# Five stacked loads a slot instead of ten, and a new order on every engine, in a one-layer decoder kernel

## The reference

```python
x = x + attn(_layernorm(x), w_qkv, w_o)              # B=4, T=512, D=512, 16 heads of 32, causal, rotary
x = x + ssm(ctx_1024, _layernorm(x), in_proj_w, ...) # selective scan, 512 channels, 16 states
x = x + ffn(_layernorm(x), w_fc, w_proj)             # 512 -> 2048 -> 512, ternary weights, GELU
# in the ssm, for each batch:
u = silu(conv(in_proj(ctx)) + conv_b);  dt, B, C = x_proj(u);  delta = softplus(dt_proj(dt) + b)
state = state * exp(delta * A) + (delta * u) * B;  y = sum_n state * C + D * u
out = y * silu(z)                                    # z is the layer-normed x after attention
```

## Time and profile before

| | |
|---|---|
| time, median of 3 runs (lowest, highest) | 1005.8 us (1002.96, 1011.9) |
| the profiled execution, own time | 1006.11 us |
| its span | 1004.2 us |
| mean granted TensorE clock | 0.964 |
| busy: TensorE, VectorE, ScalarE, GpSimd | 91%, 86%, 75%, 61% |

### The profile page before, as it was taken

How to read it: one execution, slowest core, us unless ns; L and a number is a source line. 1 busy time by engine, 2 the same in 40 slices (tenths; PEclk the granted TensorE clock), 3 DMA queues, 4 the chain that set the end, 5 groups by cost and what they waited for, 6 DMA issues and landing times.

```text
span 1004.2 us, 17516 instructions
## 1 busy us (share of the span) xinstructions
PE 913.4 (91%) x5476; PEld 605.8 (60%) x5476; DVE 859.1 (86%) x1167; ACT 757.1 (75%) x1490; POOL 617.6 (61%) x439
## 2 busy tenths in 40 slices
PE   6979898888999999989898998877999998999998
PEld 4455665666686676776666677765854554554444
DVE  4698979999999999889898678998898898899731
ACT  4987746755569878687989774996499999989660
POOL 0266927666461867687555787344579878797520
PEclk9989899999999999999999999788999999999999
DMA  5757766856564665343535466423036846574535
GB/s 167 247 190 236 215 202 206 252 165 216 158 210 141 186 209 168 113 146 103 161 96 154 120 178 246 154 64 121 6 68 153 175 98 132 121 148 84 106 74 125
DMA packets 148857, 153.57 MB, mean 153 GB/s; under 512 B 93008, under 2 KB 97360, under 8 KB 148512
## 3 DMA queue, kind: packets, MB, share of 16 engines
q1 hardware_dynamic: 148768, 152.46, 53.9%
HBM read 103.00 MB, written 28.44 MB: 131 GB/s over the span
## 4 chain that ended last, share of the span: by engine, by line
PE 41%; ACT 20%; DVE 18%; issue 12%; POOL 6%; DMA 2%; SPq 0%; ACTq 0%; DVEq 0%; POOLq 0%
PE ps L1749 6%; PE ps L1818 5%; PE ps L1875 5%; DVE hb L1895 4%; ACT p_q L1599 4%; PE ps L1830 4%; ACT ps L1486 4%; PE ps L1762 4%; PE ps L1792 4%; DVE y_acc L1917 3%; POOL hb L1366 3%; PE ps L1865 2%; ACT L1467 2%; PE ps L1773 2%; ACT p_t L1615 2%
## 5 line engine op out<-in xcount | busy, mean ns | idle before, releaser
L1366 POOL TENSOR_TENSOR hb<-du,b_bc 128x1024 f32<-128x1024 f32 (+1 forms) x160 | 307.0, 1939 | 156.7 <-PE ps L1818 156.3
L1895 DVE TENSOR_TENSOR_SCAN hb<-ps,hb 128x1024 f32<-128x1024 f32 (+1 forms) x128 | 257.2, 2015 | 20.7 <-ACT ps L1486 17.9
L1486 ACT ACTIVATE ps<-delta,a_neg 128x511 f32<-128x511 f32 (+2 forms) x320 | 179.5, 600 | 87.0 <-DVE hb L1895 81.1
L1917 DVE SCALAR_TENSOR_TENSOR y_acc<-ps,ct,y_acc 128x512 f32<-128x512 f32 x256 | 179.3, 737 | 21.4 <-PE ps L1818 21.0
L1818 PE MATMUL ps<-ident,hb 128*128 128x128 f32 x1088 | 152.0, 282 | 30.1 <-DVE hb L1895 15.9
L1818 PEld LDWEIGHTS ps<-ident,hb 128*128 128x128 f32 x1088 | 127.2, 145 | 60.6 <-issue 18.6
L1599 ACT ACTIVATE p_q<-ps,m_col 128x512 f32<-128x512 f32 (+3 forms) x256 | 132.0, 540 | 18.5 <-DVE m_col L1992 18.1
L1749 PE MATMUL ps<-xn_t,w_ring 128*128 128x512 f32 x256 | 118.0, 604 | 1.9 <-ACT p_q L1599 1.3
L1865 PE MATMUL ps<-t_fc,xt 128*128 128x512 f16 x512 | 117.1, 382 | 0.8 <-ACT h_sb L1663 0.7
L1875 PE MATMUL ps<-t_pr,ht 128*128 128x512 f16 x512 | 112.8, 379 | 1.0 <-DVE y_acc L1917 1.0
L1792 PE MATMUL ps<-ident,p_q 128*128 128x128 f32 x640 | 91.7, 295 | 8.8 <-ACT p_q L1599 6.0
(11 more groups left out here) (137 smaller groups left out, 1529.2 us busy)
## 6 DMA issues: line engine op xcount, KB each, us to landing
w_ring<-in_w_attn SPq DMA_DIRECT2D x32, 512.0 KB, 4.0
qk_d<-hl SPq DMA_DIRECT2D x64, 256.0 KB
q_st<-qk_d SPq DMA_DIRECT2D x128, 128.0 KB, 2.8
b_bc<-bc_d SPq DMA_DIRECT2D x48, 256.0 KB, 3.7
raw<-in_w_fc SPq DMA_DIRECT2D x16, 512.0 KB, 5.2
raw<-in_w_pr SPq DMA_DIRECT2D x16, 512.0 KB, 5.8
k_st<-qk_d SPq DMA_DIRECT2D x64, 128.0 KB, 2.7
k_st<-qk_d SPq DMA_DIRECT2D x128, 64.0 KB, 2.3
```

What stands on the lines that cost most here:

```text
L1366: nc.gpsimd.tensor_tensor(piece_of(e, hi, lo).rearrange("p (a n) -> p a n", a=2), du[b % 2][:, 2 * h:2 * h + 2, lo:hi], b_bc[:, i % BC_RIN ...
L1486: ins = nc.scalar.activation(factors(j, hi, lo)[:, (hi - lo) * m + start:(hi - lo) * (m + 1)], delta[b % 2][:, et, lo + start:hi], ACT.Exp ...
L1895: v.tensor_tensor_scan(h, d, h, 0.0, ALU.mult, ALU.add).then_inc(scan_done, 1)
L1917: v.scalar_tensor_tensor(out=y, in0=bank(kind, r, tb), scalar=ct[:, b % 2, tb, n:n + 1], in1=y, op0=ALU.mult, op1=ALU.add).then_inc(y_free ...
```

## The change

Each `stack` item issued five loads for each of its two heads. Now each of the five carries both heads, with the same bytes and the same rows of 2 KB, and the wait in front of the scores counts 80 where it counted 160. The planner learns that an issue keeps SyncE busy (0.46 us, and more for some kinds), where it had 0.1 us; two first loads get their real number of transfers; the factor on TensorE's and VectorE's durations goes from 1.03 to 1.02. One wait is added to the first `ln1b` copy of a batch on ScalarE, since the new order can put the last `rot` of the batch before behind the last `v`. All tables of due times have new numbers, by which every engine's order is another. What each item computes is unchanged.

```diff
-WEIGHT = {'pe': {'ln1b': 1.9,
+WEIGHT = {'pe': {'ln1b': -40.55,
...
-ATTN = [{'stack': [-7.0],
+ATTN = [{'stack': [-158.25],
...
-SWITCH = 17.35
+SWITCH = 42.4
...
+ISSUE, ISSUES = 0.46, {"xt": 1.3, "ht_ffn": 2.0, "stack": 3.4, "lo": 2.7}
...
-        yield "act", 0.5, [pe(*item)] + ([pe("v", b - 1, 1, 1)] if b else [])
+        yield "act", 0.5, [pe(*item)] + ([pe("v", b - 1, 1, 1), pe("rot", b - 1, 3, 1)] if b else [])
...
-        yield "sp", 4, [pe("inproj", a[0] - 1, ET - 1)] if a[0] else []
+        yield "sp", 4 if a[0] else 8, [pe("inproj", a[0] - 1, ET - 1)] if a[0] else []
...
-    slow = {"pe": 1.03, "dve": 1.03}
+    slow = {"pe": 1.02, "dve": 1.02}
...
-            free[engine] = at + (us if item[0] in ("xt", "ht_ffn") else 0.1)
-            line = max(line, at) + 0.72 * us
-            over[engine, item] = line + 2.2
+            free[engine] = at + ISSUES.get(item[0], ISSUE)
+            line = max(line, free[engine] - 0.45) + 0.72 * us
+            over[engine, item] = line + 1.8
...
-                    for h in range(2):
-                        head = 2 * sb_ + h
-                        q = qk_d[b, 0, head].rearrange("s p n -> (s p) n")
-                        k = qk_d[b, 1, head].rearrange("s p n -> (s p) n")
-                        for dst, rows, src in ((q_st, (0, 64), q), (q_st, (64, 128), q), (k_st, (0, 64), k),
-                                               (k_st, (64, 96), k[32:64]), (k_st, (96, 128), k[0:32])):
-                            sp.dma_start(dst[rows[0]:rows[1], p % 2, h, :].bitcast(F32), src).then_inc(stack_in[p % 2], 16)
+                    q, k = (qk_d[b, n, 2 * sb_:2 * sb_ + 2].rearrange("h s p n -> (s p) h n") for n in range(2))
+                    for dst, rows, src in ((q_st, (0, 64), q), (q_st, (64, 128), q), (k_st, (0, 64), k),
+                                           (k_st, (64, 96), k[32:64]), (k_st, (96, 128), k[0:32])):
+                        sp.dma_start(dst[rows[0]:rows[1], p % 2, :, :].bitcast(F32), src).then_inc(stack_in[p % 2], 16)
...
-                        act.wait_ge(m_full, TASK["v", b - 1, 1, 1] + 1)
+                        act.wait_ge(m_full, max(TASK["v", b - 1, 1, 1], TASK["rot", b - 1, 3, 1]) + 1)
...
-                    pe.wait_ge(stack_in[p % 2], 160 * (p // 2 + 1))
+                    pe.wait_ge(stack_in[p % 2], 80 * (p // 2 + 1))
```

More of the change, by code:

```diff
@@ L104 @@
 EARLY = 14
-WEIGHT = {'pe': {'ln1b': 1.9,
[L110 to L188, removed]
-        'xproj': -45.1,
-        'bcload': 18.0,
-        'stack': -10.5,
-        'resid': -24.2,
-        'x2store': 0.6,
-        'fwload': 24.6,
-        'fxload': -27.2,
-        'proj': -13.0}}
@@ L363 @@
[L363 to L375 removed]
+WEIGHT = {'pe': {'ln1b': -40.55,
+        'inproj': -66.23,
+        'xproj': 52.84,
+        'ct': 36.01,
+        'dt': 36.18,
+        'rot': -16.7,
+        'v': 28.68,
+        's': 10.49,
+        't': 0.51,
+        'pv': -14.56,
+        'rz': -9.8,
+        'wo': 20.24,
+        'ht': -8.38,
+        'gt': 52.57,
+        'wtot': 64.6,
+        'xt': 153.75,
+        'fc': -34.46,
+        'ht_ffn': 7.6,
+        'proj': 117.47},
+ 'act': {'carry': -68.1,
+         'exp': 22.09,
+         'skip': -67.92,
+         'ht': -65.82,
+         'ln1b': 172.89,
+         'inproj': -18.76,
+         'silu': 211.65,
+         'xproj': 105.86,
+         'ct': -129.98,
+         'dt': 57.55,
+         'hi': -102.81,
+         'v': -21.57,
+         'e': 159.23,
+         't': 95.68,
+         'pv': -37.81,
+         'rz': 34.98,
+         'gate': -16.49,
+         'xt': -4.61,
+         'ht_ffn': 14.58,
+         'fc': 15.9,
+         'wsum': 65.04,
+         'hn': -137.91},
+ 'dve': {'scan': 8.85,
+         'ht': 4.93,
+         'ln1a': 78.62,
+         'ln1b': 28.24,
+         'inproj': 96.42,
+         'delta': -78.52,
+         'rot': -74.87,
+         's': -1.64,
+         'rz': -18.35,
+         'pv': -192.46,
+         'wo': -15.0,
+         'ln2a': 23.35,
+         'ln2b': 47.13,
+         'gt': -72.13,
+         'wtot': -97.0,
+         'tern': -20.16,
+         'xa': 157.28,
+         'xc': 47.19,
+         'xt': 118.06,
+         'ht_ffn': 69.64,
+         'fc': -48.69,
+         'hstat': 223.03,
+         'hn': -111.41,
+         'hq': 17.54,
+         'proj': 159.09},
+ 'pool': {'delta': 72.43,
+          'dbu': -26.46,
+          'du': -36.26,
+          'lo': 113.37,
+          'xadd': -42.2,
+          'ln1a': -84.79,
+          'ln2a': 128.64,
+          'xa': -39.22,
+          'xc': -52.97,
+          'hstat': -183.22,
+          'rot': -14.91,
+          'xt': 51.35,
+          'ht_ffn': -79.49},
+ 'sp': {'xload': -185.09,
+        'cload': -80.68,
+        'wload': -88.67,
+        'lo': -89.88,
+        'xproj': -71.92,
+        'bcload': 100.82,
+        'stack': 114.14,
+        'resid': 7.11,
+        'x2store': 63.43,
+        'fwload': -65.57,
+        'fxload': -41.54,
+        'proj': 96.57,
+        'tstore': 61.26,
+        'twload': -63.21,
+        'xt': 86.28,
+        'ht_ffn': -16.23}}
```

317 lines of the change are left out of this document (164 added, 153 removed), and 12 rows, old and new, of tables (ATTN_END, SKIP).

## The result

The changed kernel takes **970.7 us** (median of 4 runs, 969.32 to 975.44), the kernel before, on the same chip, 1006.4 us (median of 4, 1002.96 to 1011.9). The ratio is **0.965**, with a 95% interval of 0.960 to 0.969: 35.8 us less. The forecast of 993 (12.4 us less) had the sign right and the size about a third of what came. The result lies 6 us under the low end of the range.

A forecast was written before the change was run, and what follows sets the result against it. It saw a start that waits, a middle filled by VectorE and TensorE, a TensorE-filled end, and a loose stage at 600 to 700 us set by waits. Terms 7.9 + 1.5 + 3 + 0 + 0 + 0 = 12.4 us less gave 993 us, range 977 to 1010.

The forecast's parts named there:

- the rest of the order: All engines' lists: every item moves a little, stages stay at the same places within 1%; priced at 0.
- more than the priced parts: Rival, chance 0.18: the new order fills a third of TensorE's other 82.5 us of idle time, 27 us, giving 979.
- Table loads: ScalarE: 14 fewer loads, 18.0 us of work, 44% of it on the chain of waits; 7.9 us gained (0 to 18.0).
- Loads dearer than the rows: Rival, chance 0.04: each table switch on ScalarE costs about twice as much, 15.8 us in place of 7.9, giving 985.
- The fillers: TensorE: 50 fewer fillers, 7.0 us of its time, mostly where it would have idled; 1.5 us gained.
- The clock: TensorE, 600 to 700 us, granted clock 0.90: fewer loads leave less idle and low-clock time; 3 us gained (0 to 8).
- more than 90: Expected sign: in the stage around batch 2's gates, TensorE busy over 90 us in 100, with a clock above 0.95.
- The stacked loads: SyncE: five issues a slot in place of ten, queue at 0% of the chain; 0 (2 us gain to 1 loss).
- The start: Before the first scores: first `delta` some 3 us sooner, against convolution work moved to the full middle; priced at 0.
- can't go: Start of the kernel: the first 8.3 us of TensorE's 90.8 us of idle time were held to be unavoidable.
- Too tight hand-overs: Rival, chance 0.12: TensorE waits at `s` or `t`, one more 1.09 us wait in each of 24 slots, giving 1020.
- The sign of being wrong: TensorE's idle time stays near 90 us or grows, by many short waits for ScalarE or VectorE.

The follow-up runs named there:

- a_gates: Changed kernel with batch 2's four gates spread again as in the kernel before, so six table loads more: 982.6 us, ratio 0.980.
- cut_wo2: Changed kernel's order up to the planned time of batch 2's first output projection, old order behind it, five stacked loads a slot: 988.2 us, ratio 0.985.
- a_loads: Changed kernel, no item moved, with three unneeded pairs of table loads (six loads) added on ScalarE in slots 29 to 31: 980.6 us, ratio 0.974.
- cut_s0: Changed kernel's order up to the planned time of the first scores, old order behind it, five stacked loads a slot: 999.7 us, ratio 0.995.
- b_five: Kernel before, order untouched, with five stacked loads a slot in place of ten: 1001.2 us, ratio 0.998.

## Why the prediction was right or wrong

**The step that failed is "the rest of the order", which I put at 0.** I reasoned that "the stages lie where they did ... within 1%". The four places that I compared leave out the one where the orders part, batch 2's `wo`. There the new order has begun 3193 of TensorE's 5236 matmuls without fillers where the old had 3141, one per cent more, and 76 scans where the old had 73; on VectorE's list I had not counted at all. Nor can a place in one list show whether the engines wait less for each other, and half of the profiled gain is of that kind: TensorE's idle time is 15.7 us shorter. How large this part is has a lower bound: with six of the 14 table loads put back (`a_gates`, 982.6 us) the new order still gains 22 us (ratio 0.980, 0.975 to 0.985), where the sum had 0 for it. The other eight loads were not put back.

It is the mechanism that the text named and gave 0.18, "more than the priced parts": a new order that fills a third of TensorE's idle time. It filled 15.7 us of idle time where that rival had 27, and the rest of the gain it hadn't counted: 8.4 us of busy time go with the higher clock. The range ended at 977, just below this rival's 979, and the result lies under it.

**Table loads, 7.9: wrong in kind.** Their number and time were as said, 59 and 75.7 us with the one at the very start, in the groups of after that answer to the earlier trace rows:

```profile
L1483 ACT ACT_TABLE_LOAD x28 | 35.9, 1283 | 0.5
L1679 ACT ACT_TABLE_LOAD x17 | 21.8, 1283 | 0.3
L1557 ACT ACT_TABLE_LOAD x8 | 10.3, 1283 | 0.1
L1649 ACT ACT_TABLE_LOAD x5 | 6.4, 1283 | 0.1
L1708 PE MATMUL ps<-ident 128*128 128x128 f32 x190 | 27.2, 289 | 7.2 <-DMA small<-in_small 5.9 <-ACT ct L1573 0.8 <-ACT y_acc L1536 0.2
```

Six of the 14 were taken out by themselves, at the very place that the earlier trace rows shows with its 1.87 us wait of TensorE, and gave nothing (within 3 us either way). A share of the chain (0.44) is what a group lies on, not what its removal gives. Put back into the new order, six such loads cost 10 to 12 us by themselves and 12 to 14 with the gates moved, which is as much as the loose stage's own new order brings: with the gates spread that stage takes 131.3 us, as in `cut_wo2` (130.7). So this stage's 12 us seem to need both, fewer loads and an order planned without them, and the load is no term of its own. Added loads cost 10 us in the old order too, so the price of putting them in is not the worth of leaving them out; that worth lies somewhere from 0 to 14 us, and 7.9 is neither confirmed nor refuted as a number.

**Loads dearer than the rows.** The Trainium skill (ScalarE: Activation LUTs, "What ACT_TABLE_LOAD costs") has a switch at about 2.66 us. The four gates in one run, in after, in order of time, answer to the earlier trace rows:

```profile
617.59 1.28 ACT L1649 ACT_TABLE_LOAD   x1
618.89 2.93 ACT L1649 ACTIVATE gate<-xr,nmr,rstd 128x512 f32<-128x512 f32 x4
621.84 1.28 ACT L1483 ACT_TABLE_LOAD   x1
623.13 1.30 ACT L1502 ACTIVATE ps<-delta,a_neg 128x511 f32<-128x511 f32 x2
```

There is again 0.01 to 0.02 us behind each load, and ScalarE is held for 5.5 us (5.8 was said). The trace does not agree with the page: in `a_loads` ScalarE's busy time rose by 7.8 us for six loads, 1.3 each. At the end the added pairs cost 10.1 us in the old order, 1.7 a load, and up to 2.0 in the new; part of that is TensorE's clock, so it is not a price of the load itself.

**The fillers, 1.5: not told from 0.** Leaving out all 190 of the new order changed the time by less than 1 us.

**The clock, 3 (0 to 8): too small, and too narrowly placed.** The stages before stood at 0.90 and 0.89; the same stretch of work now has 0.94, and fixed 600 to 700 us has 0.95. TensorE does it in 88.4 us of 100, not the "more than 90" that I asked for. Over the whole span it takes 8.4 us off TensorE's busy time.

**The stacked loads, 0: right.** A slot's five issues, SyncE in order of time, against the earlier trace rows:

```profile
84.52 1.33 SPq L1290 DMA_DIRECT2D q_st<-qk_d  x2
85.89 1.72 SPq L1290 DMA_DIRECT2D k_st<-qk_d  x3
```

They take 3.1 us for 6.3: for these loads SyncE pays by the issue, not by the bytes. The time at the end hardly changed (1001.2 us in the old order, and in the new one ten loads are no slower than five), as the 0% of the earlier trace rows said.

**The start, 0 (from 3 of gain to 4.6 of loss): right at the end, mis-sized on the way.** TensorE, then VectorE, in the first 60 us of after, against the earlier trace rows:

```profile
5.95 4.49 PE L1708 MATMUL ps<-ident 128*128 128x128 f32 x26 [5.95 <-DMA small<-in_small]
...
25.07 5.33 PE L1739 MATMUL ps<-du,xp_w 128*48 128x512 f32 x8 [2.64 <-ACT du L1557]
...
36.46 0.43 DVE L1973 TENSOR_SCALAR delta<-tmp 128x512 f32<-128x512 f32 x1 [8.81 <-ACT tmp L1589]
```

The first `delta` came 5.0 us sooner, where I had 3 (1.5 to 4.7), and what I had missed is in the first line: SyncE now issues the load of `small` at 2.12 us, where it did at 4.00, and the fillers start at 5.95 us, 2.4 sooner than the 8.3 of the earlier trace rows, which I had said "can't go". My 23 extra matmuls were counted ahead of `inproj`; ahead of `xproj`, which matters for `delta`, the eight transposes stood before too, and 20 more fillers do now. The first scores came 9.9 us sooner. In `cut_s0`, with the new order up to there, they came at 103.7 us and the end was within 1.5 us of `b_five`, so a gain at the end from the start alone is not shown.

**Too tight hand-overs (slower, 0.12): not seen.** TensorE's waits for `p_q` before were 24.8 us in 37 pieces (the 9.8 of the earlier trace rows among them), and are 17.1 in 28. In after the two largest sums, and the one at `s`:

```profile
PE ps L1834 <- ACT p_q L1615: 8.1, 7, 3.6
PE ps L1808 <- ACT p_q L1615: 7.7, 17, 1.5
...
PE ps L1789 <- ACT p_q L1615: 0.3, 1, 0.3
```

At `s` itself they are all but gone, 0.3 us for 9.8. The sign of being wrong, "if TensorE's idle time stays near 90 us or grows", did not come either: it is 75.1.

## What to carry to other kernels

Where each engine keeps to a fixed list, don't price a change of the plan by the instructions that it removes. Cut both orders' traces (or, before a run, both plans) at the same pieces of work and count for every engine, not TensorE alone, how much of the following stage's work is done at each cut; three scans done ahead were worth some 9 us in the next stage here, and no count of instructions shows them.

In the fixed lists of this kernel a cost was not symmetric: 7.7 to 10.3 us of work taken out of ScalarE's list gave 0 to 3 us, 7.7 us put in cost 10 to 12, and the two reorderings of TensorE's list in the middle stage cost 25 and 30. So don't expect a removal to pay while the lists stay as they are, measure it together with a new plan, and don't take the cost of putting work in for the gain of taking it out. An edit of one list "to fill a wait" can lose many times the wait.

A mixed order shows more by its trace than by its median: the place where it changes over can cost by itself, up to 7.7 us in one of these runs.

## What the runs showed of the hardware

- For these loads SyncE's cost was by the issue: ten issues of a slot (64 to 128 KB each) took 6.3 us and five of twice the size 3.1 us, about 0.6 us each. The larger ones land later, 4.3 to 4.7 us from issue to landing where it was 2.3 to 2.8, and so they do in the old order (4.1 to 4.6 in `b_five`).
- Lost clock was up to half of what a stall cost. In the stage where TensorE's list was changed alone, the same matmuls (x1072 and x1070 in the records) took 172.3 us at a granted clock of 0.91 and 155.9 at 0.99, 16.4 of the 31.7 us lost. With the six added loads it was 4.2 of 10.9 us (0.88 for 0.94).
- Filling planned idle time with transposes of the identity made no difference to the time: 971.2 us without any of the 190, 970.7 with them. The clock was 0.968 to 0.972 without and, on another chip, 0.972 to 0.979 with them.
- A table load took ScalarE 1.28 us and no more: the next activation starts 0.01 to 0.02 us behind it, and six more of them raised its busy time by 7.8 us.
